# Five of ten value products move from the prologue into filter steps, and the records that fill the sort's padding move behind every second step

## What is computed

```
xn  = layernorm(x)
x   = x + gnn(xn, src, dst, edge_attr_20, edge_weight, edge_attr_3) + linear_attention(xn)
x   = x + experts(layernorm(x))

gnn:  xs, xv = xn @ W_in2f                      # the node table, 4*128 words a node
      W  = (softplus'(f_ij @ Wf1 + bf1) @ Wf2 + bf2) * rcut     # a filter for every edge
      messages = table[src] combined with W and the edge's unit direction
      agg = segment_sum(messages, dst)          # then small mixing products
linear_attention:  q, k = softmax(xn @ Wq), softmax(xn @ Wk);  v = xn @ Wv
      context = sum_n k^T v ;  out = (q @ context) @ Wo + bo
experts: router, the two best of 8 experts for every node, expert products
```

## Time and profile before

| | us |
|---|---|
| three timed runs | 1273.39, 1271.00, 1275.69 |
| the profiled execution | 1271.56 |
| its span | 1269.5 |
| TensorE, VectorE, ScalarE, GpSimd busy | 1190.8, 1071.0, 812.4, 870.8 |

### The profile page before, as it was taken

The page is one execution under the profiler, slowest core; times in us unless marked ns, Lnnn a source line. Parts: engine busy times, 40 slices in busy tenths (PEclk is TensorE's granted clock), DMA queues, the critical chain, the costliest instruction groups (busy, mean ns, idle before and its releaser), DMA issues.

```text
span 1269.5 us, 16249 instructions
## 1 busy us (share of the span) xinstructions
PE 1190.8 (94%) x4108; PEld 700.0 (55%) x4108; DVE 1071.0 (84%) x1998; ACT 812.4 (64%) x1822; POOL 870.8 (69%) x795
## 2 busy tenths in 40 slices
PE   4999999989999999899999999999999999977995
PEld 3566666767766664344444444444444444766882
DVE  5958999899989995699999999999999997589325
ACT  3667777777767660576776767767767674775330
POOL 6357777777777775688888888888888881053650
PEclk8989999999999999899999999999999999987996
DMA  9248876887799966988888898988898881554557
GB/s 276 63 153 298 296 266 256 314 304 270 291 320 358 305 236 233 351 302 309 316 309 307 305 315 305 311 309 302 315 309 304 310 265 34 203 188 143 183 172 235
DMA packets 106608, 337.65 MB, mean 266 GB/s; under 512 B 16783, under 2 KB 17803, under 8 KB 100373
## 3 DMA queue, kind: packets, MB, share of 16 engines
q0 software_dynamic: 57264, 188.75, 41.5%
q1 hardware_dynamic: 49252, 147.88, 35.4%
HBM read 211.27 MB, written 125.30 MB: 265 GB/s over the span
## 4 chain that ended last, share of the span: by engine, by line
PE 76%; DVE 12%; DMA 4%; issue 3%; ACT 2%; POOL 1%; SPq 0%; DVEq 0%; POOLq 0%; ACTq 0%
PE PS L2306 22%; PE PS L2311 22%; PE PS L2242 11%; PE PS L2431 6%; DVE RR L1587 4%; PE PS L2109 3%; PE PS L2119 2%; PE PS L2087 2%; DMA X<-in_x 1%; DMA edge_records<-RR 1%; DVE h_low L1580 1%; PE PS L2240 1%; PE PS L2409 1%; POOL edge_records L953 1%; PE PS L2202 1%
## 5 line engine op out<-in xcount | busy, mean ns | idle before, releaser
L990 POOL DMA_INDIRECT RR<-node_table,RR x322 | 445.4, 1383 | 112.2 <-issue 64.0
L1250 ACT ACTIVATE RR<-RR 128x256 f32<-128x256 f32 x966 | 394.5, 494 | 194.1 <-PE PS L2311 155.6
L953 POOL DMA_INDIRECT edge_records<-RR x316 | 315.0, 997 | 107.3 <-issue 72.7
L2306 PE MATMUL PS<-RR 128*125 128x512 f32 x644 | 291.6, 595 | 3.8 <-DVE RR L1765 3.7
L2311 PE MATMUL PS<-RR 128*125 128x512 f32 x644 | 289.6, 592 | 0.0
L2306 PEld LDWEIGHTS PS<-RR 128*125 128x125 f32 x644 | 121.0, 189 | 162.1 <-issue 144.4
L2311 PEld LDWEIGHTS PS<-RR 128*125 128x125 f32 x644 | 120.9, 188 | 155.5 <-issue 155.5
L1587 DVE TENSOR_TENSOR RR<-PS,RR 128x512 f32<-128x512 f32 x237 | 161.0, 687 | 23.4 <-PE PS L2242 22.7
L2242 PE MATMUL PS<-wf_high,h_high 128*128 128x512 f32 x316 | 148.5, 470 | 8.7 <-DVE RR L1587 8.4
L1765 DVE TENSOR_TENSOR RR<-RR 128x1536 f32<-128x1536 f32 (+1 forms) x81 | 141.0, 1741 | 0.0
L2242 PE MATMUL PS<-wf_low,h_high 128*128 128x512 f32 x316 | 125.9, 398 | 0.0
(11 more groups left out here) (354 smaller groups left out, 1799.1 us busy)
## 6 DMA issues: line engine op xcount, KB each, us to landing
RR<-edge_records SPq DMA_DIRECT2D x48, 1040.0 KB, 6.6
expert_inputs<-RR SPq DMA_DIRECT2D x8, 2313.0 KB, 17.7
RR<-edge_records SPq DMA_DIRECT2D x27, 520.0 KB, 5.1
RR<-edge_records SPq DMA_DIRECT2D x15, 780.0 KB, 5.5
RR<-in_L_ffn_beta_w SPq DMA_DIRECT2D x8, 1024.0 KB
expert_w_raw<-in_L_ffn_expert_w SPq DMA_DIRECT2D x8, 1024.0 KB, 7.0
RR<-edge_records SPq DMA_DIRECT2D x31, 260.0 KB, 5.2
edge_records<-RR POOLq DMA_INDIRECT x322, 4.3
```

What stands on the lines that cost most here:

```text
L953: g.indirect_dma_start(out=rec_dram, out_offset=place, in_=ST[:, j, :], in_offset=None).then_inc(scattered[c], 16)
L990: g.indirect_dma_start(out=GB[q % GBS][:, t, 1:5, :].rearrange("p k n -> p (k n)"), out_offset=None, in_=tab_dram, in_offset=bass.Indirect ...
L1250: last = a.activation(message_slot(q)[:, t, k:k + 5:4, :], GB[q % GBS][:, t, 0:k + 3:k + 2, :], ACT.Copy, scale=record_slot(q)[:, t, 4 * C ...
L2306: te.matmul(PS[0:NT, 2 * (r % PSS), :], OH[q % OHS][:, t, 0:NT], GB[q % GBS][:, t, 1:5, :].rearrange("p k n -> p (k n)"), start=(n == 0), ...
```

## The change

Three things move; no arithmetic changes.

1. **Values.** FRONT = 5 value products stay in the prologue. The other five run in the steps with r = 5 of tiles 0 to 4 (steps 8, 14, 20, 26 and 32): two of the four matmuls behind the step's first filter, one behind the second, one behind the fourth. They use PSUM bank 6 between the query's transposes and the next query, so the first of them waits for `copy_qT` and the next query waits for the copy of the values, which ScalarE makes at the start of the next step. The weight Wv is loaded a second time (`WV_again`), since its first place has become part of the ring.
2. **Prologue.** The last tiles' transposes and table products alternate with the first steps' first-layer rows on TensorE, ScalarE and VectorE. VectorE's `places_in_blocks` is cut in three, with `hidden` and `low` of the first steps between. `block_bases` comes earlier, the reciprocal of the edge lengths (L1549) much earlier. The first features are loaded behind the first-layer weights and ahead of Wq and Wk. The wait for the stored table rows moves from step 0 to step 3.
3. **Padding.** The six `spare_record` scatters stand behind steps 1, 3, 5, 7, 9 and 11. The blank rows can only begin when they have landed: BLANK_STEP goes from 3, 18, 34, 50 to 16, 27, 37, 50. GpSimd's constants for later stages move behind `spare_places`.

The core of the diff:

```diff
+        FRONT = 5
+        EARLY_XT = 6
+        SPARE_STEPS = range(1, 1 + 2 * (NCOL - LOOPED), 2)
-        BLANK_STEP = [TILE_STEP] + [2 * CHUNK * k + 2 for k in range(1, BLANKS)]
+        BLANK_STEP = [SPARE_STEPS[-1] + 5, 27, 37, 50]
@@ SyncE
-            load_projection(WQ, Wq, wqkv_in[0])
-            load_projection(WK, Wk, wqkv_in[1])
-            load_features(0)
-            load_features(1)
...
+            load_features(0)
+            load_projection(WQ, Wq, wqkv_in[0])
+            load_projection(WK, Wk, wqkv_in[1])
+            load_features(1)
...
+            sp.wait_ge(edge_places, 2)
+            load_projection(WV_again, Wv, wqkv_in[2])
@@ GpSimd
-            for n in range(NCOL - LOOPED):
-                spare_record(LOOPED + n)
             pool.wait_ge(edge_places, 2)
             for m in range(STEPS):
                 scatter(m // RING, m % RING)
+                if m in SPARE_STEPS:
+                    spare_record(LOOPED + SPARE_STEPS.index(m))
@@ ScalarE, filters(i, c)
+                if r == 0 and 1 <= t <= NB - FRONT:
+                    values(FRONT + t - 1)
@@ ScalarE, behind the radial rows of the first steps
             radial(0, 0)
             stage_f(2)
+            table_rows(6)
+            evac_xT(7)
             log_part(0, 0)
             radial(0, 1)
+            stage_f(3)
+            table_rows(7)
+            evac_xT(8)
+            log_part(0, 1)
             high(0, 0)
...
+            table_rows(8)
+            evac_xT(9)
+            bias_rows()
+            table_rows(9)
+            log_part(0, 2)
             radial(0, 3)
@@ VectorE
+            places_in_blocks(range(0, 3))
+            hidden(0, 0)
             stage_f_low(0, 2)
-            hidden(0, 0)
-            dve.wait_ge(b2_ready, 1)
-            low(0, 0)
-            stage_f_low(0, 3)
-            hidden(0, 1)
-            stage_f_low(0, 4)
+            places_in_blocks(range(3, 6))
+            low(0, 0)
+            hidden(0, 1)
+            stage_f_low(0, 3)
+            places_in_blocks(range(6, NB))
+            edge_rows()
+            stage_f_low(0, 4)
+            dve.wait_ge(b2_ready, 1)
             dve.wait_ge(dirs_ready, 1)
-            dve.wait_ge(v_psum, NB)
-            for s in range(2):
-                dve.wait_ge(tab_out[s], 32 * (NB // 2))
+            dve.wait_ge(v_psum, FRONT)
             stage(0, 0)
@@ TensorE
+            def late_value(t, k):
...
+                if k == 0:
+                    pe.wait_ge(qT_ready, t - FRONT + 1)
+                last = te.matmul(PS[0:NT, value_bank(t), :], XTQ[:, t, k, :], WV_again[:, k, :], start=(k == 0),
+                                 stop=(k == KD - 1))
...
-                elif 0 <= t < NB and r == PER - 1 and j == 2:
-                    context(t)
+                elif 0 <= t < NB and r == PER - 1:
+                    if j == 2:
+                        context(t)
+                    elif t < NB - FRONT:
+                        for k in ((0, 1), (2,), (), (3,))[j]:
+                            late_value(FRONT + t, k)
```

More of the change, by code:

```diff
@@ L338, in gps_layer @@
         assert c1_early <= c2.at - 2 * P and c2.at <= acc_at
-        in_hidden = 4 * 512 // RC1
-        mask_at = [hidden_at + b * RC1 if b < in_hidden else kn_at + (b - in_hidden) * RC1 for b in range(NB)]
-        assert c1_early <= hidden_at and (NB - in_hidden) * RC1 <= 3 * D
+        FRONT = 5
+        in_values = (NB - FRONT) * D // RC1
+        mask_at = [vn_at + FRONT * D + b * RC1 if b < in_values else kn_at + (b - in_values) * RC1 for b in range(NB)]
+        assert c1_early <= hidden_at and (NB - in_values) * RC1 <= 2 * D
         block_mask = [R1[:, w:w + RC1] for w in mask_at]
@@ new lines, in _ @@
+            table_rows(2)
+            evac_xT(3)
+            moments_of((6, 7))
+            values(2)
+            table_rows(3)
+            evac_xT(4)
+            moments_of((8, 9))
+            later_std(slice(6, NB), NB - 1)
+            a.preload_act_table_set("natural_log_exp_and_others")
+            rounded_weights()
+            stage_f(0)
+            stage_f(1)
+            values(3)
+            table_rows(4)
+            evac_xT(5)
+            values(4)
+            table_rows(5)
@@ L1380, in statistics, with inverse_lengths @@
                 step(v.tensor_copy(mean[0:NT, cols], aggr[0:NT, cols, 0]))
+            def inverse_lengths():
+                dve.wait_ge(nrm_root, 1)
+                v.reciprocal(inv, inv).then_inc(nrm_inv, 1)
             def inverse_root(ts, part):
@@ L1559, in stage @@
                     dve.wait_ge(scattered[c], i * (16 * STEP))
+                elif c == 2:
+                    dve.wait_ge(tab_psum, NB)
+                elif c == 3:
+                    for s in range(2):
+                        dve.wait_ge(tab_out[s], 32 * (NB // 2))
                 v.tensor_copy(ST[:, c * STEP:(c + 1) * STEP, 4 * C:REC], meta[:, cols, :]).then_inc(staged, 1)
@@ L2076, in table_product @@
                 for k in range(KD):
-                    last = te.matmul(PS[0:NT, 2, k * C:(k + 1) * C], XTQ[:, t, k, :], wsv[:, min(k, 1), :],
+                    last = te.matmul(PS[0:NT, table_bank(t), k * C:(k + 1) * C], XTQ[:, t, k, :], wsv[:, min(k, 1), :],
                                      start=True, stop=True)
@@ L2089, in value_product, with block_counts @@
                 last.then_inc(v_psum, 1)
-            for t in range(NB - 1):
-                if t == 2:
-                    transpose_x(2)
-                table_product(t)
-                if t >= 2:
-                    transpose_x(t + 1)
-                if t < NB - 2:
-                    value_product(t)
-                if t == COUNT_TILE:
-                    pe.wait_ge(counts_ready, NB)
-                    te.matmul(PS[:, 7, 0:NB], ltri[:, :], cnt, start=True, stop=True)
-                    te.matmul(PS[:, 7, NB:2 * NB], ones[:, 0:P], cnt, start=True, stop=True).then_inc(counts_psum, 1)
+            def block_counts():
+                pe.wait_ge(counts_ready, NB)
+                te.matmul(PS[:, 5, 0:NB], ltri[:, :], cnt, start=True, stop=True)
+                te.matmul(PS[:, 5, NB:2 * NB], ones[:, 0:P], cnt, start=True, stop=True).then_inc(counts_psum, 1)
+            def late_value(t, k):
+                if t == FRONT and k == 0:
+                    pe.wait_ge(wqkv_in[2], 64)
+                if k == 0:
+                    pe.wait_ge(qT_ready, t - FRONT + 1)
+                last = te.matmul(PS[0:NT, value_bank(t), :], XTQ[:, t, k, :], WV_again[:, k, :], start=(k == 0),
+                                 stop=(k == KD - 1))
+                if k == KD - 1:
+                    last.then_inc(v_psum, 1)
+            table_product(0)
+            value_product(0)
+            table_product(1)
+            value_product(1)
+            transpose_x(2)
+            table_product(2)
+            transpose_x(3)
+            value_product(2)
+            table_product(3)
+            transpose_x(4)
+            value_product(3)
+            table_product(4)
+            transpose_x(5)
+            value_product(4)
+            table_product(5)
+            transpose_x(6)
+            block_counts()
             def query(t, k):
```

162 lines of the change are left out of this document (80 added, 82 removed).

## The result

| | before | after |
|---|---|---|
| median of the timed runs, us | 1273.39 (15 runs, 1269.19 to 1276.24) | 1276.3 (15 runs, 1272.6 to 1278.92) |
| ratio after / before | | 1.0024, 95% interval 1.0015 to 1.0034 |
| profiled execution, us (span) | 1271.56 (1269.5) | 1276.24 (1274.5) |

The changed kernel is a little slower, by 2.9 us of medians, inside what the forecast called no change. A second series gave 1.0022 (1.0006 to 1.0039). The profiles differ by more, 4.7 us, because that of before is an execution 1.8 us under its median and that of after stands on its median.

The account below looks back on a forecast made before the run. GpSimd's scatter line races TensorE and VectorE's pace, which decides only where GpSimd runs dry, last at step 28. There -9.8 + 8.4 + 5.5 = +4.1 us, giving 1276 us; own range 1272 to 1280, eight in ten 1266 to 1282.

Parts of the forecast that it names:

- The prologue: Before the filter steps: with five value products moved out, the first scatter comes 9.8 us earlier, allowed 8 to 12.
- It is the engine that ends the prologue: End of the prologue: VectorE, no longer TensorE, finishes last, with the places ready at about 67.3 us.
- A value product in a step: Steps with r = 5: each late value product adds 2.1 us on TensorE; four before the scatter of 229.86 add 8.4.
- The feature wait: Step 19: ScalarE waits 5.5 us for the fourth chunk's features, queued behind blank rows; the wait passes whole to TensorE.
- Rival 3's sign: VectorE's staging waits for scatters between 155 and 190 us, showing a slower queue: 1282 us, chance 0.18.
- The queue argument: SyncE's queue, around step 16: descriptors go in ring order, so blank rows hold the features back; otherwise 5.5 us less.
- From there both kernels scatter without a wait: Behind the scatter of 229.86, step 28: GpSimd never runs dry again, so the stage's end follows 263.9 us later.
- covered by backlog: Step 32: the fifth late value product costs nothing, since GpSimd was 5 us behind the filters at 254.90.
- The padding records: Early filter steps: six scatters add 7.9 us to GpSimd's line, which with gaps filled ends at -4.4 us.
- The sum: At the scatter of 229.86: -9.8 + 8.4 + 5.5 = +4.1 us, holding against -4.4 for GpSimd's own line.
- The clock argument: First filters: more TensorE idleness ahead makes them run at 1.2 GHz, some 2 us; at most 1 us of the sum.
- I count the same there as before: TensorE's clock at 75 to 91.5 us, granted 0.86 and 0.74 beside small matmuls, is taken as unchanged.

Follow-up runs that it names:

- second profile: The changed kernel run once more without any edit, for another profile: 1276.03 us, ratio 1.0022 to the kernel before; its profiled execution took 1271.48 us.
- short values: The changed kernel with three of the four matmuls of each late value product left out: 1269.54 us, ratio 0.9978 to the kernel before.

## Why the prediction was right, and where its steps were not

The total, 1276.0 against 1276.3, is right. It is the sum of errors that cancel, and so partly luck: the last scatter, forecast near 498, came at 498.39 in the profile of after but at 495.34 in its second profile.

- **The prologue: right, 1 us small.** -10.9 for -9.8. The places were not the last: staged at 64.63, not 67.3, and VectorE then waited 1.54 us for ScalarE. "It is the engine that ends the prologue" fell; the filters' own chain does.
- **A value product in a step: right.** 1.8 to 1.95 us each in the first four, forecast 2.1. The short values show that it goes with TensorE's matmuls and lies on the filters' line.
- **The feature wait: the right place, mis-sized, and one face of two.** 5.5 us forecast, 3.16 in the first profile, none in the second. The term that was off is the landing: I took the last blank DMA's from other places of before (17.0 to 20.8 us) and had the features land no sooner, 18 us or more after their issue, where they took 14.4 to 16.6; in the second profile that blank DMA landed after 14.4. GpSimd did not run dry behind the wait either, as the forecast's sign had it: at step 20 both lines stood at -3.9. Rival 3's sign, VectorE waiting for scatters between 155 and 190 us, appeared with it or instead of it (2.24 and 1.06 us), at a fraction of its price. The queue argument fits: with the blank rows back in step 3 both waits are gone and some 4 us are won, with only the features moved ahead the feature wait is gone.
- **"From there both kernels scatter without a wait": wrong.** I named the last dry place by the trace of before, step 28. When the filters' line had lost its lead, VectorE's run tables in step 38, hidden before behind GpSimd's backlog, ran it dry. The fifth value in step 32, "covered by backlog", was therefore not covered, as I read it: the filters' line stood at +1.94 behind it, and GpSimd went from -0.7 at step 38 to +1.4 at step 39. Moving the tables shows their part; no run takes the fifth value alone away.
- **The padding records: half wrong.** The line's sum of +7.9 less the gaps was right, but I counted it as nothing against a later filters' line. Padding and blank rows alone cost 6.2 us; with padding in front the ratio is 2 us better, inside the noise. When GpSimd is late the ring fills, VectorE waits for landings and the filters' line is pushed back as well. The two lines don't race; they hold each other, and a dry place later adds up what both lost.
- **The sum.** Forecast at step 28: +4.1. Measured there: -1.7 for GpSimd, -0.4 for the filters. The missing 4.5 us came back as the fifth value (2.4), and as 3.3 us between step 39 and the last scatter. These are longer scatters, nearly all: from the first of step 39 to the last GpSimd's gaps sum to 49.1 us in both kernels, its scatters to 158.0 us before and 161.2 after. So the wait before 295.39 (0.86 us) made no difference to before in the end. The sum had no term for this, and how much of it is the change's is open: in the second profile of after the same stretch has 159.5 us of scatters and 51.1 of gaps.

The clock argument was half right. TensorE idled 3.26 us ahead of 58.90 and was granted half the clock from 59.86 to 63.26, where before ran at 1.00. But the first filter's first three matmuls start at 64.29 to 64.75 and took 0.39 to 0.40 us each, the length at full clock:

```profile
60.00:65.00 5.00, 4.75 (x24) 3.87 (x23) 4.62 (x12) 2.85 (x6) 1.96 (x14) 0.67 0.17 51
65.00:70.00 5.00, 3.52 (x20) 2.71 (x19) 3.52 (x7) 4.90 (x11) 1.20 (x1) 1.00 0.77 261
```

This cost next to nothing: in the second profile of after the stretch from 60 to 65 us ran at 1.00, and the first scatter came at 68.46 for 68.61. The Trainium skill's rule (TensorE: Matmul & The Clock Gate, part 1: a fall after idleness, a rise with activity) agrees with these two rows.

"I count the same there as before" was where the clock mattered. The second profile of after has no low stretch at 77 us, behind the same narrow matmuls:

```profile
75.00:85.00 10.00, 10.00 (x60) 8.01 (x59) 6.57 (x17) 6.56 (x14) 7.68 (x8) 1.00 0.67 246
```

Its filters' line stands 1.6 us ahead of the first profile's from step 3 on (-12.36 against -10.77). So one low stretch of 3.4 us among the filters is worth 1.4 to 1.6 us of a step's difference, and it comes and goes between executions of one kernel. What decides that, no run here shows.

## What to carry to other kernels

Where an engine with a backlog hides others' work, a dry place is not a property of the place but of the backlog: after a change that uses the lead up, look for the longest gap in the feeding engine that was hidden before, and not only for the old dry place. Work moved between a producer and a consumer that hold each other through a ring is charged to both lines. And a part that frees the start (here -0.27%) can be undone by a part that only makes room for it (+0.49%): try them apart, since the version with padding and blank rows left where they were beats both kernels.

## What the runs showed of the hardware that I had not expected

- Two experts' blank rows issued back to back, 4.6 MB in their two large stores, delay other traffic of the same 20 us. The features, issued between them, took 14.4 to 16.6 us to land; scatters, which are another queue's, took 6.5 to 9.4 us in place of 2.7 to 3.7. What that costs depends on the slack of those who wait: 3.16 us or none for the features in two executions of one kernel, 1.6 or 3.3 for VectorE. The Trainium skill (DMA: Bandwidth & Descriptors, section on queues, rings and completion order) says that a semaphore increment lands only after every earlier write of that DMA engine, across its queues; the landing waits agree with it, though no run here separates this from mere sharing of bandwidth. Of such a wait, read the landing time and the slack, each by itself, and not the wait alone.
- A scatter's issue on GpSimd takes 0.96 us or, in 39 of 316 before and 51 after, more, up to 1.5 us. A long one began while VectorE ran a wide operation with two tensor operands and none in PSUM: 587 of 662 such scatters with 0.22 us or more of the operation left, against 1 of the 2665 that began beside an idle VectorE or an operand in PSUM. The Trainium skill (GPSIMD Engine Reference, its table of trn2 properties) says that GpSimd's SBUF interfaces are shared with VectorE, with contention for VectorE instructions that have two SBUF inputs or are in what it calls a 2-port perf mode. These counts agree with the first; whether the 14 of 52 with one SBUF operand are the second, the traces don't say.
- TensorE was granted half the clock for 3.4 us in the steps of some executions and not of others of the same kernel, behind the same work: at 77 us once of two, behind the 2.9 us of idleness in step 38 once of two.
- The first scatter of one and the same prologue came at 69.5 and at 71.5 us, one profile each.
